# A graph kernel of four layers on one core: adj^T read from a turned copy in HBM, or turned afresh in SBUF by VectorE in 32x32 pieces

## The reference

```python
# layer 0
e = concat(par_u0*par_u1*(diag_u*x_u @ W_u) + x_u, par_i0*par_i1*(diag_i*x_i @ W_i) + x_i)
h = adj @ (adj.T @ e)
x = ln(x + (h - mean(h)) * rsqrt(var(h) + 1e-5) * gamma + beta + x)
# layer 1
x = ln(x + 1 - 0.1*x - 0.01*sum(x * (adj @ x), axis=1))
# layer 2
deg = clip(sum(adj, axis=1) + 1, 1)
z = relu(concat(x, (adj @ x + x)/deg) @ W + b)
x = ln(x + z / max(norm(z), 1e-12))
# layer 3
T1 = adj @ x;  T2 = 2*(adj @ T1) - x;  T3 = 2*(adj @ T2) - T1
x = ln(x + x@w0 + T1@w1 + T2@w2 + T3@w3 + bias)
```

## Time and profile before

| | |
|---|---|
| median of 3 runs | 1672.71 us (1662.72 to 1673.04) |
| span of the profiled execution, first to last instruction | 1666.0 us |
| TensorE, VectorE, ScalarE busy | 1605.0, 776.5, 420.1 us |
| moved from and to HBM | 411.69 MB read, 106.17 MB written |
| mean granted TensorE clock | 0.991 of 2.4 GHz |

### The profile page before, as it was taken

How to read it: one execution, slowest core, us unless ns; L and a number is a source line. 1 busy time by engine, 2 the same in 40 slices (tenths; PEclk the granted TensorE clock), 3 DMA queues, 4 the chain that set the end, 5 groups by cost and what they waited for, 6 DMA issues and landing times.

```text
span 1666.0 us, 20499 instructions
## 1 busy us (share of the span) xinstructions
PE 1605.0 (96%) x6938; PEld 828.1 (50%) x6938; DVE 776.5 (47%) x1334; ACT 420.1 (25%) x651; POOL 61.6 (4%) x66
## 2 busy tenths in 40 slices
PE   7999999999999999999999989999999999999998
PEld 5656666665665653333444434444444444444433
DVE  5788888888888887423321243222210011100232
ACT  2466666666666650000000000000000000000000
POOL 0000000000000002100000010000000000000010
PEclk9999999999999999999999999999999999999999
DMA  9999999999999987999788757787278866888896
GB/s 322 410 363 336 336 347 343 332 350 337 339 352 334 333 301 286 420 421 408 256 287 291 277 204 276 282 290 286 77 268 289 312 240 256 301 313 292 325 402 263
DMA packets 118187, 518.63 MB, mean 311 GB/s; under 512 B 15692, under 2 KB 16884, under 8 KB 68084
## 3 DMA queue, kind: packets, MB, share of 16 engines
q1 hardware_dynamic: 102048, 412.66, 67.7%
q10 hardware_dynamic: 16084, 105.23, 16.6%
HBM read 411.69 MB, written 106.17 MB: 311 GB/s over the span
## 4 chain that ended last, share of the span: by engine, by line
issue 99%; POOLq 0%; POOL 0%; DVE 0%
POOL power_out L396 0%; POOLq L394 0%; POOLq L396 0%; DVE rows L840 0%; POOL ident L389 0%; POOLq L391 0%; POOL ident L391 0%; POOLq L1035 0%
## 5 line engine op out<-in xcount | busy, mean ns | idle before, releaser
L447 ACT ACTIVATE at_raw<-ps_turn 128x512 f32<-128x512 f32 x400 | 206.6, 604 | 214.4 <-DVE at_lo L740 189.0
L664 PE MATMUL ps_back<-at_raw,vectors 128*128 128x512 f32 (+1 forms) x592 | 242.4, 596 | 1.0 <-DVE part L985 1.0
L765 DVE TENSOR_REDUCE row_part<-nat 128x2048 f32 (+1 forms) x100 | 228.1, 2281 | 1.0 <-issue 0.2
L664 PE MATMUL ps_u<-at_raw,vectors 128*128 128x512 f32 (+1 forms) x648 | 223.5, 600 | 3.2 <-DVE part L996 3.2
L539 PE MATMUL ps_turn<-ident,nat 128*128 128x128 f32 x1600 | 200.8, 279 | 20.4 <-ACT at_raw L447 10.3
L740 DVE TENSOR_TENSOR at_lo<-at_raw,at_hi 128x1024 fp32r<-128x1024 f32 x180 | 211.7, 1218 | 0.2 <-ACT at_hi L425 0.2
L539 PEld LDWEIGHTS ps_turn<-ident,nat 128*128 128x128 f32 x1600 | 176.2, 141 | 52.9 <-ACT at_raw L447 37.2
L551 PE MATMUL ps_u<-nat,e 128*64 128x512 f32 x800 | 193.7, 605 | 0.0
L425 ACT ACTIVATE at_hi<-at_raw 128x1024 fp32r<-128x1024 f32 x180 | 182.2, 1076 | 8.9 <-PE ps_h L509 8.2
L664 PE MATMUL ps_back<-at_more,vectors 128*128 128x512 f32 (+1 forms) x408 | 160.3, 595 | 0.0
L461 ACT ACTIVATE part<-ps_h 128x512 f32<-128x512 f32 x40 | 23.9, 597 | 540.7 <-PE ps_h L664 540.7
(11 more groups left out here) (100 smaller groups left out, 935.3 us busy)
## 6 DMA issues: line engine op xcount, KB each, us to landing
at_raw<-a_transposed SPq DMA_DIRECT2D x170, 1024.0 KB, 5.3
at_more<-a_transposed SPq DMA_DIRECT2D x121, 1024.0 KB, 5.4
nat<-in_adj SPq DMA_DIRECT2D x100, 1024.0 KB, 6.0
a_transposed<-at_raw ACTq DMA_DIRECT2D x100, 1024.0 KB, 4.3
out<-rows SPq DMA_DIRECT2D x10, 128.0 KB, 3.5
rows<-in_x SPq DMA_DIRECT2D x1, 128.0 KB, 2.4
twice<-in_L_gnn_weight ACTq DMA_DIRECT2D x6, 16.0 KB, 6.1
vec<-in_L_gnn_ln_gamma ACTq DMA_DIRECT2D x1, 32.0 KB, 5.5
```

The source lines that it names most:

```text
L447: nc.scalar.activation(at_raw[:, i, t, :], ps_t[t][:, :], ACT.Copy)\
L664: mm = pe.matmul(acc, left, tiles[:, t, :], start=first, stop=last)
L765: V.reduce_sum(row_part[:, i * TB:(i + 1) * TB, bass.ds(j, 1)].rearrange("p t o -> p (t o)"), nat[:, i % NAT], AX.X).then_inc(nat_summed, 1)
```

## The change

There is no `a_transposed` and no float32r part any more. All blocks, for adj^T e too, come from adj, and stage 1 and stage 2 become one list.

- **First pass.** u = adj^T e is computed in ten pieces k of 512 rows. For each, the ten blocks of one column of adj ("NAT" blocks) are loaded as they are; TensorE multiplies the pieces of e by them (`row_block`, L525), adding into one bank. After each piece VectorE copies the bank (`copy_u`), TensorE turns it (`turn_u`, in the middle of the next block) and VectorE stores it as a vector (`end_u`); the BEGIN blocks of a row of h = adj * u follow as soon as their pieces of u are there. h is thus the first of six products that the triangular sweeps serve in place of five (s = 0 to 6), and there is one more whole sweep, whose turns are `end_l0`. Row sums are shared: VectorE sums two of a block's four parts, ScalarE the other two.
- **Turning.** For adj * v the 512x512 block is loaded with its 512-byte pieces in such an order that one VectorE instruction over 128 x 2048 (`V.transpose`, in place, 32x32 pieces; L621) leaves it as adj^T up to an order of columns that TensorE's operand undoes by its strides. The rows of x, out and diag are dealt to partitions in the matching order.
- **Loads.** A load is four DMAs, one for each 32 partitions: SP issues those for partitions 0 to 63, ACT those for 64 to 127. For a NAT block the pieces are runs of 2 KB, for a block to be turned they are runs of 512 bytes. There are 16 slots; the load for a block may begin at the earliest when the block 6 places ahead in the list is done (`APART`), and VectorE's turning of it stands in VectorE's program 3 blocks ahead of its use (`LEAD`; one block earlier inside some norms, `turn_spare`).

The list has 490 blocks in place of 332, and 423 loads: 100 NAT, and 323 with 512-byte runs. 156 blocks (100 NAT, 55 BEGIN, 1 END, with 156 loads) precede the point where sweep 0's last row is kept; five whole sweeps with 44, 46, 44, 46 and 44 loads follow, and then 44 END blocks with 43 loads.

```diff
-    at_dram = nc.dram_tensor("a_transposed", [NB, NB, P, TB * BLK], F32, kind="Internal").ap()
-    a_blocks = adj.rearrange("(t p) j -> p t j", p=P)
+    adj_rows = adj.rearrange("(i a c y) j -> i a y c j", a=Q, c=TB, y=QP)
+    adj_quarters = adj.rearrange("(i b y) (j a w) -> i j a y b w", b=BLK // QP, y=QP, a=Q, w=P)
+        for k in range(NB):
+            for i in range(NB):
+                blocks += [(0, k, i, NAT)]
+            then("u", 0, k, mid)
+            if k > 0:
+                blocks += [(0, k - 1, q, BEGIN) for q in range(k)]
+                then("keep", 0, k - 1)
...
+                    n = max((n for n in range(SLOTS) if holds[n][2] <= b - APART),
+                            key=lambda n: (again[holds[n][2]], -holds[n][2]))
+                    free_at = holds[n][2] + 1
...
+        def load_quarters(eng, n, quarters):
+            need, slot, _, _, free_at = loads[n]
+            if free_at > 0:
+                eng.wait_ge(block_done, free_at)
...
+            for a in quarters:
+                if need[0] == "rows":
+                    dst = blk[quarter(a), slot].rearrange("p (c j) -> p c j", c=TB)
+                    src = adj_rows[need[1], a, :, :, need[2] * BLK:(need[2] + 1) * BLK]
+                else:
+                    dst = blk[quarter(a), slot].rearrange("p (b w) -> p b w", w=P)
+                    src = adj_quarters[need[1], need[2], a]
+                eng.dma_start(dst, src).then_inc(loaded[slot], 16)
...
+            def row_block(b):
...
+                tiles = blk[:, loads[n][1]].rearrange("p (t a c y) -> p t c a y", t=TB, a=Q, c=TB)
+                for t in range(TB):
+                    mm = pe.matmul(ps_both[k % 2][half(t), :], e_rows[:, i * TB + t, :], tiles[:, t],
...
             def multiply_block(b):
+                pe.wait_ge(turned, turn_no[load_of[b]] + 1)
...
+                tiles = blk[:, slot_of[b]].rearrange("p (a d c y) -> p c d a y", a=Q, d=TB, c=TB)
...
+            def turn_next():
+                n = to_turn[n_done[0]]
+                slot = loads[n][1]
+                dve.wait_ge(loaded[slot], n_loaded(n))
+                V.transpose(blk[:, slot], blk[:, slot]).then_inc(turned, 1)
+            def turn_due(b):
+                while n_done[0] < len(to_turn):
+                    n = to_turn[n_done[0]]
+                    if max(loads[n][3] - LEAD, begin_at[n]) > b:
+                        break
+                    turn_next()
...
+            for b in range(len(blocks) + 1):
+                turn_due(b)
+                for what, s, r in after.get(b, ()):
```

More of the change, by code:

```diff
@@ L28 @@
 F32 = mybir.dt.float32
-F32R = mybir.dt.float32r
 ALU = mybir.AluOpType
@@ L183, in build @@
         block = ctx.enter_context(nc.Block())
-        N_CONSTS, N_WEIGHTS = 6, 16
+        N_CONSTS, N_WEIGHTS = 4 + NB, 16
         N_ROOTS = 6 * NB
-        BASES = (1, 2)
+        BASES = (2, 3)
         def at(s, r):
             return NB - 1 - r if s % 2 == 0 else r
-        BOTH, END, BEGIN = range(3)
+        BOTH, END, BEGIN, NAT = range(4)
         blocks = []
@@ L214, in build @@
             if s == 0:
-                for r in range(NB - 1):
-                    blocks += [(s, r, q, BEGIN) for q in range(r + 1)]
-                    then("keep", s, r)
                 blocks += [(s, NB - 1, q, BEGIN) for q in range(NB - 1)]
@@ L276, in build @@
                     events.append(("base", s, r))
-        group = [("own" if which == BEGIN else "both", s, r) for s, r, q, which in blocks]
+        group = [("u", s, r) if which == NAT else ("own" if which == BEGIN else "both", s, r)
+                 for s, r, q, which in blocks]
         def opens(b):
@@ L324, in raw @@
-        def raw(slot):
-            return at_raw[:, slot] if slot < NB else at_more[:, slot - NB]
+        needs = [("rows", q, at(s, r)) if which == NAT else ("turned", at(s, r), at(s, q))
+                 for s, r, q, which in blocks]
+        never = len(blocks)
+        again, seen = [never] * len(blocks), {}
+        for b in range(len(blocks) - 1, -1, -1):
+            again[b] = seen.get(needs[b], never)
+            seen[needs[b]] = b
+        holds = [None] * SLOTS
+        loads, slot_of, load_of = [], [], []
@@ new lines, in build @@
+        n_in_slot = [0] * SLOTS
+        for b, need in enumerate(needs):
+            here = [n for n in range(SLOTS) if holds[n] is not None and holds[n][0] == need]
+            if here:
+                n = here[0]
+                load_of.append(holds[n][1])
+            else:
+                empty = [n for n in range(SLOTS) if holds[n] is None]
+                if empty:
+                    n, free_at = empty[0], 0
+                else:
+                    n = max((n for n in range(SLOTS) if holds[n][2] <= b - APART),
+                            key=lambda n: (again[holds[n][2]], -holds[n][2]))
+                    free_at = holds[n][2] + 1
+                n_in_slot[n] += 1
+                load_of.append(len(loads))
+                loads.append((need, n, n_in_slot[n], b, free_at))
+            slot_of.append(n)
+            holds[n] = (need, load_of[b], b)
@@ new lines, in build, with n_loaded @@
+        begin_at = [max(free_at for _, _, _, _, free_at in loads[:n + 1]) for n in range(len(loads))]
+        turn_no, n_turned = {}, 0
+        for n, (need, _, _, _, _) in enumerate(loads):
+            if need[0] == "turned":
+                turn_no[n] = n_turned
+                n_turned += 1
+        row_blocks = [b for b in range(len(blocks)) if blocks[b][3] == NAT]
+        sum_no = {b: k for k, b in enumerate(row_blocks)}
+        def n_loaded(n):
+            return 16 * Q * loads[n][2]
@@ new lines, in sum_rows @@
+            def sum_rows(b):
+                n = load_of[b]
+                s, k, i, _ = blocks[b]
+                act.wait_ge(loaded[loads[n][1]], n_loaded(n))
+                if sum_no[b] > 0:
+                    act.wait_ge(summed_act, sum_no[b])
+                for c in range(HT):
+                    add = nc.scalar.activation(junk[:, c], blk[:, loads[n][1], c * BLK:(c + 1) * BLK], ACT.Copy,
+                                               accum_out=row_part[:, i * TB + c, k:k + 1])
+                add.then_inc(summed_act, 1)
@@ L798, in _, with turn_spare @@
+            def turn_spare(b):
+                if n_done[0] < len(to_turn):
+                    n = to_turn[n_done[0]]
+                    if begin_at[n] <= b and loads[n][3] - LEAD - 1 <= b:
+                        turn_next()
             roots = [0]
```

616 lines of the change are left out of this document (230 added, 386 removed).

## The result

The changed kernel takes 1938.8 us, median of 4 runs (1934.6 to 1946.8), against 1672.9 us for the kernel before (4 runs, 1662.7 to 1673.6). The ratio is 1.162, with a 95% interval of 1.157 to 1.166. The forecast was 1712 us, and its range ended at 1880.

What follows compares the result with a forecast made beforehand. It took DMA to bound the first pass and TensorE a sweep. First pass 498, five sweeps 1011, waits from VectorE's queue 62 and last stretch 134 gave a 1705 us span, 1712 us as median; range 1610 to 1880.

Steps and rivals of the forecast that it cites:

- Price of a load: All loads: 3.6 us for one to be turned, 2.73 us for a NAT one; wrong if below 2.9 or above 4.
- So it lands 0.85 us after b has begun: Rows 4 to 8 of sweeps: a load lands 6.0 us after beginning, 5.15 us before b; TensorE then waits 2.3 us.
- made up for: Long rows of sweeps: a load per block costs 3.6 us against the block's 3.43, and turns absorb the difference.
- The wait for `add_y`: Sweeps 1 to 4: TensorE waits for add_y, 44 us in 19 rows and 8 us at four row-9 turns.
- VectorE's order: Sweeps: VectorE turns the block for place b+3 ahead of add_y at b, so a late landing delays add_y; 2.3 us a row.
- First pass: Until sweep 0's last row is kept: DMA bounds it, 498 us against 754.7 before; bounds 438 and 540.
- Last stretch: The 44 END blocks after the sweeps: 33 loads at 3.6 us plus 15 us after the last transfer, 134 us.
- That VectorE doesn't hold TensorE: Rival, sweeps: loads land 2 us sooner than 6.0, so the wait is gone; 1650 us, chance 15%.
- that short runs are cheap: Rival, loads: 512-byte runs cost little more than long ones, 2.65 us a load; 1605 us, chance 12%.
- that turning takes 4.6 us: Rival, VectorE: turning takes two cycles an element, 247 us of VectorE in a sweep; about 1900 us, chance 7%.
- That quarters collide: Rival, loads: DMAs to quarters of the partitions hinder each other, with a 12% loss; 1789 us, chance 17%.
- Its worst case: Rival, loads: one queue's half proceeds while the other's waits, 4.8 us for any load; about 2100 us, chance 9%.

Runs made afterwards that it cites:

- apart9: The changed kernel with APART 9 in place of 6, so loads may begin three blocks earlier: 1791.7 us.
- add_first: The changed kernel with add_y and copy_u ahead of the turnings due at the same block in VectorE's program: 1839.0 us.
- tiny_turn: The changed kernel with VectorE turning only 128x128 of each block's 128x2048, so values are other ones: 1844.6 us.
- pairs: The changed kernel with SP loading partitions 0 to 31 and 64 to 95, ACT 32 to 63 and 96 to 127: 2239.0 us.
- one_queue: The changed kernel with all four DMAs of a load issued by SP, none by ACT: 2296.5 us.
- wide2: The changed kernel with each load DMA writing a fourth of the bytes of all 128 partitions, from other rows of adj: 1823.7 us.
- a12_dve_keep: The changed kernel with APART 12, add_y and copy_u ahead of turnings, and keep_own's copy moved from ACT to VectorE: 1771.4 us, ratio 1.064.

## Why the prediction was wrong

- **Price of a load: right for turned ones at a full queue.** 3.61 us against 3.6, 290 GB/s, and 2303 ns for the turning against 2.3. With one load under way it was 4.24, which passes the 4 us that the forecast named as its sign of being wrong. NAT loads: 3.05 against 2.73, because of the quarters, 99 x 0.32 = 32 us; over all partitions they took 2.71.
- **The step that failed** is "So it lands 0.85 us after b has begun", with its 6.0 us from begin to landing. It took each load by itself. In a long row a load begins at nearly every block, 3.43 us apart, and each costs 4.24 while the queues are short; so one that finds another under way lands 7.8 us after its begin, with two 9.9, with three 12.3. The sentence that 3.6 against 3.43 is "made up for" by the turns hid the same thing. The wait for `add_y` was at the right place and not far off in size, 64.0 us in sweeps 1 to 4 against 52. But with landings that late the turnings ahead of `keep_both` are late too: 55.9 us there, for which the forecast had no term, and 15.6 for turned blocks, where it had 9 at slow ends and in short rows. The five sweeps came to 148 + 62 = 210 us beyond the 1011, where the upper bound was 110. apart9 shows that lateness is the cause: with three blocks more of lead the sweeps take 1086 us. That is near the 1073 forecast only by luck, since the 62 us of waits in it are not the ones that are left.
- **A term that was missing**: the clock. 27.5 of sweep 4's 58.5 extra us are slower matmuls, at 1.2 GHz after waits.
- **VectorE's order**, named as the mechanism, held: 71 us in the sweeps if it alone is mended, but only 11 once the loads have lead.
- **First pass**: 566.2 against 498. 32 us are NAT loads; the landings show 7.0 us behind the loads of x, 5.2 where all 16 slots are full, and 34 at other places, most of it at the ten pieces of u, where 9 were forecast; 4.4 follow the last landing.
- **Last stretch**: 146.1 against 134; add_first and tiny_turn (134.9, 125.0) put the 11 us on VectorE's queue, which the forecast had left out here (TensorE waited 33.6 us for `add_y` in this stretch).
- **The rivals.** That VectorE doesn't hold TensorE, that short runs are cheap, and that turning takes 4.6 us are refuted by their own numbers. That quarters collide was true, and I priced it as a loss on every load; it is one on NAT loads (3.05 us against 2.71) and on short queues (4.24 against 3.69), and none at a full queue of turned loads. Its worst case, 4.8 us for any load, is what pairs and one_queue have (4.3 to 4.9), and the change avoids it by giving each queue its own half.
- **Small slips in the sums**: the terms of the 62 us give 61; 32 x 84 ns is 2.69 us, not 2.65; and half the rate of rows 6 and 8, 205 GB/s, would be 5.1 us a load, not 4.8. None changes the outcome.
- With the loads' lead, the order and `keep_own` mended, the forecast span of 1705 would still have been 52 us low: 58 in the first pass and 4 at the end, against 10 too many in the sweeps.

## What to carry to other kernels

Time a load by the queue that it meets: from begin to landing it took 6.4 us here with nothing ahead of it and 12.3 with three loads ahead, and if one is issued per block and costs more than the block, the lag grows along the row until some gap lets it catch up. Ask first how far ahead the program lets a load begin; here one constant, 6 to 9, was worth 147 us, more than any other single edit. When TensorE is made to wait often for short times, count the slower clock after them: in sweep 4 it cost nearly as much again as the waits. And where a DMA must cover a part of the partitions, let one of the two queues write to 0 to 63 while the other writes to 64 to 127.

## What the runs showed of the hardware

- Two queues with 2 KB runs moved 347 GB/s into quarters of different halves, 224 into quarters of the same half, 387 over all partitions; with 512-byte runs 288 in the first case (1600 to 1700 of the changed kernel) and 291 in the last (1500 to 1600 of wide2).
- A DMA whose source begins with a dimension of 4 ran on 4 of 16 engines: 102 GB/s, and the first pass took more than twice its time.
- A DMA share near 1 (0.83 to 0.89 in sweeps 1 to 4) went with 180 to 192 GB/s, where a full queue moved 290. With two queues the share adds both: it read 1.2 at that rate.
- 32x32 transposes of 128x2048 floats in place took 2303 ns, about as long as the reduction over the same shape, 2280.
- Short waits of TensorE lowered its clock: mean granted 0.89 in sweep 4 with 31.8 us of idle time, 1.00 in the same sweep of a12_dve_keep with 1.6.
